# Gated experts of the first layer: routing weights spread over partitions by DMA and multiplied in by GpSimd, instead of by TensorE products and a VectorE multiplication

## The reference

```python
combine = (jax.nn.one_hot(tki, E, dtype=tkw.dtype) * tkw[..., None]).sum(1)
g = jax.nn.silu(jnp.einsum('th,eih->tei', h, w_gate))
u = jnp.einsum('th,eih->tei', h, w_up)
routed = jnp.einsum('tei,ehi->th', g * u * combine[:, :, None], w_down)
sg = jax.nn.silu(h @ sh_gate.T)
shared = sg * (h @ sh_up.T) @ sh_down.T
return (routed + shared).reshape(B, S, Hd)
```

## Time and profile before

| what | value |
|---|---|
| three runs | 3299.76, 3303.3, 3305.57 us; median 3303.3 us |
| the profiled execution | 3299.01 us, span 3297.2 us |
| TensorE (PE) | busy 2813.7 us, 85% of the span |
| VectorE (DVE) | busy 2196.5 us, 67% |
| ScalarE (ACT) | busy 1846.6 us, 56% |
| GpSimd (POOL) | busy 1497.0 us, 45% |
| DMA | 208.30 MB, mean 63 GB/s |
| stage out0 | from 1298.9 us of the span |
| stage experts0 | from 1393.7 to 1720.4 us, its loop from 1404.0 us |

### The profile page before, as it was taken

The page is one execution under the profiler, slowest core; times in us unless marked ns, Lnnn a source line. Parts: engine busy times, 40 slices in busy tenths (PEclk is TensorE's granted clock), DMA queues, the critical chain, the costliest instruction groups (busy, mean ns, idle before and its releaser), DMA issues. The chain is left out here.

```text
span 3297.2 us, 68039 instructions
## 1 busy us (share of the span) xinstructions
PE 2813.7 (85%) x21529; PEld 1319.4 (40%) x21530; DVE 2196.5 (67%) x3330; ACT 1846.6 (56%) x3190; POOL 1497.0 (45%) x1114
## 2 busy tenths in 40 slices
PE   5999999999999996899984599999996942676994
PEld 2333333333333333833333122222225942664772
DVE  5666666666666662988886899999982347535663
ACT  4555555555555552054456299999993654255432
POOL 1899999999999996500001011110112534541000
PEclk7999999999999997999996699999998975787995
DMA  2111111111111112600002312112214661262002
GB/s 82 32 50 44 50 53 44 44 50 44 58 45 44 50 44 91 227 1 1 0 2 97 92 41 51 43 45 50 45 40 147 188 207 35 72 178 60 11 13 58
DMA packets 275320, 208.30 MB, mean 63 GB/s; under 512 B 148846, under 2 KB 210726, under 8 KB 274320
## 3 DMA queue, kind: packets, MB, share of 16 engines
q1 hardware_dynamic: 266992, 192.77, 20.4%
q0 software_dynamic: 8224, 14.24, 1.3%
HBM read 125.43 MB, written 66.77 MB: 58 GB/s over the span
## 5 line engine op out<-in xcount | busy, mean ns | idle before, releaser
L604 DVE TENSOR_REDUCE attn_half_max<-attn_peek 128x2 f32<-128x1024 f32 x504 | 617.8, 1226 | 452.1 <-PE attn_peek L415 448.4
L353 POOL TENSOR_TENSOR attn_esum<-attn_esum,attn_prob 128x1024 f32<-128x1024 f32 x384 | 904.2, 2355 | 30.6 <-ACT attn_prob L521 4.6
L521 ACT ACTIVATE attn_prob<-attn_score 128x1024 f32<-128x1024 f32 x512 | 512.5, 1021 | 299.0 <-PE attn_score L389 297.1
L961 DVE TENSOR_REDUCE attn_half_max<-attn_peek 128x2 f32<-128x1024 f32 x512 | 584.0, 1215 | 13.7 <-PE attn_peek L880 13.7
L944 ACT ACTIVATE attn_prob<-attn_score 128x512 f32<-128x512 f32 x1024 | 556.3, 596 | 65.5 <-PE attn_score L894 51.3
L447 PE MATMUL attn_acc<-attn_prob,attn_v 128*64 128x512 f32 x2048 | 489.1, 599 | 0.1
L910 PE MATMUL attn_acc<-attn_prob,narrow_v 128*32 128x256 f32 x4096 | 330.1, 394 | 12.0 <-ACT attn_out L936 10.5
L1829 POOL DMA_INDIRECT sorted_x<-attn_sent_rows,attn_send x64 | 62.5, 976 | 562.2 <-PE attn_score L894 562.2
L880 PE MATMUL attn_peek<-narrow_ke,narrow_qe 48*128 48x512 bf16 x1024 | 204.3, 396 | 26.3 <-DVE attn_half_max L961 14.8
L447 PEld LDWEIGHTS attn_acc<-attn_prob,attn_v 128*64 128x64 f32 x2048 | 131.2, 137 | 208.0 <-issue 163.5
L894 PE MATMUL attn_score<-narrow_qe,narrow_ke 49*128 49x512 bf16 x1024 | 201.8, 391 | 7.8 <-ACT attn_prob L944 6.5
(11 more groups left out here) (558 smaller groups left out, 4324.0 us busy)
## 6 DMA issues: line engine op xcount, KB each, us to landing
experts_w<-in_L_ffn_W SPq DMA_DIRECT2D x80, 256.0 KB, 2.7
attn_xb<-attn_x_all SPq DMA_DIRECT2D x64, 256.0 KB, 2.6
attn_invB<-inv SPq DMA_DIRECT2D x64, 256.0 KB, 3.9
o<-attn_out SPq DMA_DIRECT2D x32, 512.0 KB, 2.7
out_o<-o SPq DMA_DIRECT2D x8, 2048.0 KB, 7.8
experts_w<-in_L_ffn_w SPq DMA_DIRECT2D x40, 256.0 KB, 2.7
mix_f<-picked SPq DMA_DIRECT2D x16, 512.0 KB, 7.2
experts_x<-sorted_x SPq DMA_DIRECT2D x112, 65.0 KB, 2.2
```

The costliest lines, as they stand in the source:

```text
L353: nc.gpsimd.tensor_tensor(own, before, prob[:, u % NPROB, :, :], ALU.add).then_inc(added, 1)
L521: nc.scalar.activation(prob[:, u % NPROB, :, :], score[:, u % 2, :, :], ACT.Exp).then_inc(exped, 1)
L604: V.tensor_reduce(half_max[:, :, t, half], first_look(m) if first else peek[:], AX.X, ALU.max, negate=True).then_inc(maxed, 1)
L961: V.tensor_reduce(half_max[:, half, PAIR * pair:PAIR * (pair + 1), t], peek[:, m % NPEEK, :, :], AX.X, ALU.max, negate=True).then_inc(maxe ...
```

## The change

The routing weights are kept in float32 and no longer split. In out0 TensorE turns them four tiles at a time (32 instructions as before, now float32 and 32 rows out), ScalarE copies them out of PSUM in eight pieces (`share`), and SyncE writes them to a DRAM scratch `share0` of 32 by 4096 in two halves, after the weight loads and ahead of the powers' stores. GpSimd's `gated_sel` is gone, as are VectorE's split and copies.

In experts0 SyncE reads, for each of the 128 routed pieces, two rows of 512 weights from `share0`, each into 64 partitions of a slot of `rep` (256 KB written), six slots ahead. GpSimd multiplies `a` by `rep` into `g`, VectorE makes `h` from up and `g` in one instruction, and the seventh product of a piece is gone. The bank 1 of `up` has four slots instead of two, `a` and `g` three, the halves of `h` four; down products run three pieces behind instead of two; the sums use two banks in turn, and the copy to `fT` comes at piece 6 of the next chunk. The PSUM banks of `rep` went to these. The loop is written out in full on every engine.

```diff
@@ project_and_route_stage @@
+            for n in range(2):
+                own = slice(n * TOK // 2, (n + 1) * TOK // 2)
+                sp.wait_ge(share_copied, (n + 1) * NT // TURN // 2)
+                sp.dma_start(gated.share_d[:, own], share[:, own]).then_inc(share_out, DMA)
             job.store(sp)
             sp.wait_ge(gated_in, gated.LOADS * DMA)
+            sp.wait_ge(share_out, 2 * DMA)
...
-            gated.select(pool, made, 3)
...
-                pe.wait_ge(parts_ready, 1)
+                pe.wait_ge(share_ready, 1)
                 for t in range(NT):
-                    if t % 8 == 0 and t >= 16:
-                        pe.wait_ge(b_copied, t // 8 - 1)
-                    last = nc.tensor.transpose(trb[:, t // 8 % 2, t % 8, :], parts[:, t, :, :].rearrange("p a e -> p (a e)"), ident16[:])
+                    n, own = t // TURN, slice(t % TURN * P, (t % TURN + 1) * P)
+                    if t % TURN == 0 and n >= 2:
+                        pe.wait_ge(share_copied, n - 1)
+                    last = nc.tensor.transpose(turned[:, n % 2, own], pick[:, t, :], ident[:])
...
+            for n in range(NT // TURN):
+                act.wait_ge(share_turned, n + 1)
+                nc.scalar.activation(share[:, n * TURN * P:(n + 1) * TURN * P], turned[:, n % 2, :], ACT.Copy).then_inc(share_copied, 1)
...
-            split_weights()
...
-            for n in range(NT // 8):
-                dve.wait_ge(b_turned, n + 1)
-                V.tensor_copy(cT[:, n * 8 * P:(n + 1) * 8 * P].rearrange("r (t p) -> r t p", p=P), trb[:, n % 2, :, :]).then_inc(b_copied, 1)
@@ gated_experts_stage @@
+    TURNS, MADE, HELD, SPREAD, LAG = 4, 3, 4, 6, 3
...
+            for m in range(NCH * NSEL):
+                i, k = divmod(m, NSEL)
+                if m >= SPREAD:
+                    sp.wait_ge(shared, m - SPREAD + 1)
+                sp.dma_start(rep[:, m % SPREAD, :],
+                             share_d[2 * k:2 * k + 2, i * CH:(i + 1) * CH].unsqueeze(1).to_broadcast([2, P // 2, CH])
+                             ).then_inc(rep_in[m % SPREAD], DMA)
...
+        @block.gpsimd
...
+                pool.wait_ge(rep_in[m % SPREAD], DMA * (m // SPREAD + 1))
+                pool.wait_ge(acted, n + 1)
+                if n >= MADE:
+                    pool.wait_ge(mixed, n - MADE + 1)
+                nc.gpsimd.tensor_tensor(g[:, n % MADE, :], a[:, n % MADE, :], rep[:, m % SPREAD, :], ALU.mult).then_inc(shared, 1)
...
+            def down(n):
+                i, k = divmod(n, HT)
+                pe.wait_ge(h_split, n + 1)
+                if k == 0 and i >= 2:
+                    pe.wait_ge(copied, i - 1)
...
+                if n >= 2:
+                    pe.wait_ge(acted, n - 1)
+                product(up[0][:, n % 2, :], up_w[0], own, x_parts, (slice(None), tok), True, True).then_inc(first_up, 1)
+                if n >= TURNS:
+                    pe.wait_ge(mixed, n - TURNS + 1)
+                product(up[1][:, n % TURNS, :], up_w[1], own, x_parts, (slice(None), tok), True, True).then_inc(second_up, 1)
+                if n >= LAG:
+                    down(n - LAG)
...
-                    if k < NSEL:
-                        V.tensor_tensor(g[:, s, :], up[1][:, s, :], a[:, s, :], ALU.mult).then_inc(tmp_ready, 1)
-                        dve.wait_ge(tmp_ready, i * NSEL + k + 1)
-                    V.scalar_tensor_tensor(out=h[:, s, :], in0=(rep if k < NSEL else up[1])[:, s, :], scalar=H_SCALE / UP,
-                                           in1=(g if k < NSEL else a)[:, s, :], op0=ALU.mult, op1=ALU.mult).then_inc(mixed, 1)
+                V.scalar_tensor_tensor(out=h[:, n % 2, :], in0=up[1][:, n % TURNS, :], scalar=H_SCALE / UP,
+                                       in1=(g if routed else a)[:, n % MADE, :], op0=ALU.mult, op1=ALU.mult).then_inc(mixed, 1)
```

More of the change, by code:

```diff
@@ L1637, in down, with body @@
                         k == 0, k == HT - 1).then_inc(summed, 1)
-            def body(i, slot, first):
-                tok = bass.ds(i * CH, CH)
-                if not isinstance(i, int):
+            def body(n, i, k):
+                tok, own = slice(i * CH, (i + 1) * CH), slice(k * P, (k + 1) * P)
+                if i == 2 and k == 0:
                     pe.wait_ge(x_split, NX)
-                for k in range(HT):
-                    s = (slot * HT + k) % 2
-                    n = i * HT + k
-                    own = slice(k * P, (k + 1) * P)
-                    if not (first and k < 2):
-                        pe.wait_ge(acted, n - 1)
-                    product(up[0][:, s, :], up_w[0], own, x_parts, (slice(None), tok), True, True).then_inc(first_up, 1)
-                    if not (first and k < 2):
-                        pe.wait_ge(mixed, n - 1)
-                    ins = product(up[1][:, s, :], up_w[1], own, x_parts, (slice(None), tok), True, True)
-                    if k < NSEL:
-                        ins = nc.tensor.matmul(rep[:, s, :], sel[:, own], cT[:, tok], start=True, stop=True)
-                    ins.then_inc(second_up, 1)
-                    if not (first and k < 2):
-                        c, m, other = before(i, k, 2)
-                        down(c, slot ^ other, m)
@@ L1664, in _ @@
+                if n >= LAG:
+                    down(n - LAG)
+            iterations(body)
+            for n in range(NCH * HT - LAG, NCH * HT):
+                down(n)
         @block.scalar
@@ L1707, in _, with body @@
-            iterations(act, body)
-            high(NCH - 1, 1, HT - 1, True)
+                nc.scalar.activation(fT[:, i * CH:(i + 1) * CH], acc[:, i % 2, :], ACT.Copy, scale=1.0 / (H_SCALE * W_SCALE)).then_inc(copied, 1)
+            def body(n, i, k):
+                act.wait_ge(first_up, n + 1)
+                if n >= MADE:
+                    act.wait_ge(mixed, n - MADE + 1)
+                nc.scalar.activation(a[:, n % MADE, :], up[0][:, n % 2, :], ACT.Silu, scale=1.0 / UP).then_inc(acted, 1)
+                if piece_at(i, k) is not None:
+                    split_high(piece_at(i, k))
+                if n:
+                    high(n - 1)
+                if k == 6 and i:
+                    copy_out(i - 1)
@@ L1709, in _ @@
+            iterations(body)
+            high(NCH * HT - 1)
             copy_out(NCH - 1)
@@ L1759 @@
+            iterations(body)
+            low_part(NCH * HT - 1)
 class ExpertWeights:
```

163 lines of the change are left out of this document (57 added, 106 removed).

## The result

The changed kernel takes 3648.7 us (median of four runs, 3646.2 to 3649.0), the kernel before 3301.5 us beside it (3299.5 to 3305.6): a ratio of 1.105, 95% interval 1.103 to 1.107. It is slower by 347 us; 3262 us was forecast. The profiled execution took 3648.95 us, with a span of 3647.2.

What follows compares the result with a forecast made beforehand. TensorE looked like the bound, but not purely: 0.16 us a piece were waits. Loop -35.9 and out0 -4.5 made -40.4 us, from 3303.3 to 3262.9, said as 3262 us; range 3245 to 3288 us.

Steps and rivals of the forecast that it cites:

- The spreads: experts0: 128 spreads of 256 KB, one per 2.16 us or 122 GB/s, hidden by six slots; a like spread ran at 320.
- Rival C: experts0: the spreads bound; one after another at 3.9 us, loop 499 us, kernel 3482 us; chance 0.06.
- Loop: experts0, first product to last copy: 316.35 us falls to 280.5, -35.9 us, bounds -48 and -20.
- TensorE's floor: experts0: nine products make 1.95 us a piece, 265 us for 136 pieces, plus 3 for the end: 268 us.
- Two banks: experts0: with the sums in two banks, TensorE's waits at the chunks' edges go, 6.7 us in all.
- GpSimd's 1.27 us: experts0: GpSimd's 128x512 multiplication, interpolated at 1.27 us once per piece, bounds 1.18 and 1.47; fits into 1.95.
- The shared way: experts0: GpSimd's multiplication and VectorE's low half exclude each other, 1.67 us a piece with 0.14 overlaps; delay, no rate bound.
- Rival A: experts0: the low half does not exclude GpSimd; loop 268 us, kernel 3251 us; chance 0.2.
- The chain: experts0: waits for the shared way use up the low half's 1.1 us slack; 0.08 us lost, 2.03 a piece.
- the forecast's own 3 and 1.5 us: experts0: 3 us for the loop's end, 1.5 for twelve low parts of later tokens in chunks 0 and 1.
- Rival B: experts0: exclusion bites fully, 2.15 to 2.2 us a piece, loop 296 to 303, kernel 3278 to 3286; chance 0.15.
- out0: Stage out0: -4.5 us, bounds 0 and -7; turning -2.6, last sum -1.3, earlier start 0.5; `share` landing just covered.

Runs made afterwards that it cites:

- e1: Changed kernel with each spread as two DMAs of one row, partitions outermost, instead of one DMA with two rows outermost: 3270.2 us, 0.991 of the kernel before.
- e2: Changed kernel with spreads of half the bytes (256 columns, used twice by GpSimd), still one DMA each: 3341.5 us, one run.
- e5: e1 with four copies outermost and 16 inside in each row's DMA: 3318.0 us, one run.
- e10: e1 with eight copies outermost and 8 inside in each row's DMA: 3273.7 us, one run.
- e12: e6 with high and low halves made a piece later, three `h` slots, down products five behind, six slots for halves: 3260.1 us, 0.987 of the kernel before.
- e11: e1 with VectorE's low half reading `up` in PSUM instead of `h` in SBUF (wrong values): 3260.8 us, one run.
- e8: Kernel before the change, with only the sums in two banks and their copy at piece 6: 3291.7 us, ratio 0.9975.
- e6: e1 with down products four pieces behind, five slots for the halves of `h`, four for `a` and `g`: 3257.8 us, 0.988 of the kernel before.
- e9: e6 with down products five pieces behind and six slots for the halves of `h`: 3268.6 us, 0.992 of the kernel before.

## Why the prediction was wrong, and where it was right

**The step that failed is "The spreads".** It put 128 spreads at 122 GB/s under the 320 GB/s of the earlier trace rows, and called them hidden. Those rows show two DMAs of one head each, with the 64 partitions outermost. The change has one DMA with the two rows outermost. It ran on two engines at 51 GB/s, 5.16 us a spread, and 128 of these are 660 of the loop's 666 us. e1 changed this shape alone and gave 378 us back; e2, e5 and e10 show that the price goes with the bytes per engine, and the engines with the outermost dimension, up to the rate that the loop asks for. The forecast compared bytes and sources of the two spreads, not their shapes; the diff had the shape in plain sight.

The Trainium skill says this (DMA: Bandwidth & Descriptors, "Why a DMA increments its semaphore by 16 and not by 1"): the number of engines is the largest number up to 16 that divides the slowest dimension, other than 1, of both sides; its "Rules for kernel authors" add that a leading broadcast of c copies confines the DMA to at most c engines. By that rule it is 2 engines for the change, 16 for e1, 4 for e5 and 8 for e10. This case's trace agrees: shares of 2.1 and 4.3 engines in the change and in e5, and more than eight packets at once for 5% of the time in e10 and for 39% in e1.

**Rival C** named the bound and its break-even (2.48 us a spread, 106 GB/s). The break-even held, between e5's 102 and e10's 120 GB/s. Its signs came too: GpSimd waits for DMA. Its price, 3482 us from 3.9 us one after another, was a time to landing and not the time that a spread holds its engines, which was 5.16. Its chance of 0.06 leant on the same rows as the step above.

**With e1, the other steps can be held against a run.** It took 3270.2 us, inside the range, 8 above the forecast.
- *Loop*: forecast 280.5 with bounds of 268 and 296, measured 288.4.
- *TensorE's floor*: 268; e12 and e11 reached 268.3 and 266.6.
- *Two banks*: 6.7 us of waits; e8 gave 7.5.
- *GpSimd's 1.27 us*: 1.263.
- *The shared way*: right in kind. VectorE's scalar_tensor_tensor is held as the TENSOR_TENSOR of the earlier trace rows was. In e1's timeline the low half starts at 1500.14, the multiplication ends at 1500.80, and the low half at 1501.35; less its own 0.68 it began in effect at 1500.67, 0.13 before the other's end. The forecast had 0.14.
- *Rival A*, no exclusion, falls: the low half has a mean of 1258 ns, and e11, which removes what the two share, is 22 us shorter.
- *The chain*: wrong by its size. Less the forecast's own 3 and 1.5 us, e1's 288.4 are 2.09 us a piece instead of 2.03. It followed the low half to TensorE and found the slack just used up, which e6 confirms (60.5 us of TensorE's waits in e1, 10 us of loop). It did not follow the delayed `h` on: through the high half into ScalarE's queue, where silu of n+2 stands behind it, back to GpSimd. This round of 4.11 us for two pieces is the rest; of the kernels that keep the exclusion only e12, which opens it and gives the slack too, reaches the floor. Rival B had such a mechanism but through TensorE, with 2.15 to 2.2 a piece.
- *out0*: -3.7 us instead of -4.5, near by luck, since two terms are off against each other. The turning took 4.8 us (5.5 forecast). The products behind it took 7.31 us where the forecast kept 8.74: before, TensorE had waited 4.42 us for VectorE's copies, and its granted clock was 0.83 from 1381.0 to 1389.8; in the change it was 1.00. So VectorE was done 6.0 us earlier, where the forecast's terms make 4.4. But `share` was not covered. The last completions of the weight loads and of `share` among the trace's packets come at 1386.7, 4.9 us behind the last weight load's issue where the forecast had 4, and the next stage starts 1.55 us behind them; in e1, e2 and e5 this distance is 1.53 each time. That the landing of `share` sets the end is read from these distances, and no run tests it.

The Trainium skill (SBUF — State Buffer, "Who interferes with whom") calls the contention on the shared ports an exclusive lock, by which, as an estimate, a piece would hold the way for 1.27 + 0.68 = 1.95 us. In e1 the two overlap by 0.13 us at a handover, so the measurement decides for slightly less; that an instruction of VectorE with two SBUF inputs contends with GpSimd's, the trace agrees for scalar_tensor_tensor too.

**A version that beats both kernels** is e6: 3257.8 us, 0.988 of the time before and 391 us under the change. e12 has the shorter loop, but a whole that can't be told from it.

## What to carry to other kernels

When the time of a transfer is taken from another one in the trace, compare the outermost dimension of both sides, and not only bytes, source and number in flight; a DMA with two rows outermost ran at 51 GB/s where the same bytes with 64 partitions outermost gave the 120 the loop asked for. In a profile where everything waits, follow the waits to the one whose releaser is a DMA, and read the DMA share times 16 as a number of engines. And when a delay is laid on an instruction, follow it round the queues of all engines that stand behind it: if it comes back to its start, its round divided by the pieces in it bounds the loop, and more slack towards the last engine does not help.

## What was not expected of the hardware

**SyncE is held at the issue.** With two engines carrying the spreads, SyncE's issue took 5.04 us (median) instead of 0.59. A long issue time is then no price of issuing; it says that the transfers ahead of it have not got on.

**TensorE stands still in a later stage, and its clock falls behind that.** In the attention stage that comes behind the loop, e12's profiled execution has three places where TensorE does nothing for 4.4 to 4.8 us and no release ends it that the profile shows ("issue"). The first of them in the timeline, and all three in the waits of 1880 to 2380:

```profile
1957.72 0.61 PE L894 MATMUL attn_score<-narrow_qe,narrow_ke 49*128 49x512 bf16 x2 [4.35 <-issue]
...
PE attn_score L894 <- issue: 13.8, 3, 4.8
```

Behind each the granted clock falls to half, 1.2 GHz, for 3.4, 6.8 and 10.2 us, from 1957.8, 2036.3 and 2118.2 us on. In e6, e1 and before there is no such place, and the clock stays at 2.4 GHz for some 590 us there. The windows of 500 us of e12 and of e6:

```profile
1880.00:2380.00 500.00, 472.35 (x4920) 134.42 (x4916) 475.00 (x462) 455.05 (x847) 50.99 (x54) 0.98 0.21 46
```

```profile
1880.00:2380.00 500.00, 483.55 (x5108) 139.74 (x5108) 492.65 (x479) 471.86 (x878) 52.18 (x55) 1.00 0.21 47
```

In the same time e12 gets through 4920 products and e6 through 5108, 3.7% fewer. From its first `attn_score` product to its last the stage takes 629.1 us in e12 and 608.0 in e6, which is 21 of the 32 us by which e12's rest is longer. The profiled executions of all kernels sort the same way: two standstills in e11 (621.5 us), one each in e10 and e2 (616.3 and 616.5), none in the other nine (608 to 611), and from 30 us behind the stage's start to its end the clock fell behind these standstills and nowhere else. So one costs 6 to 7 us, clock and all. How busy the loop kept TensorE does not sort them: in the windows of 100 us it was 100 in e11 and e12, but 98 in e10 and 81 in e2, and 99.6 in e6 and e9, which have no standstill. It is also part of why e11's kernel, with the shortest loop, took 3260.8 us. Only one execution of each kernel has a profile; that the spread of e9's times (3252 to 3275 us) and of e12's has this source would fit, and is not shown. What makes TensorE stand still there stays open.
